# A mixture-of-experts block around attention: the first routing renumbered and regrouped, six weight splits moved into the expert loop

## Chip, cores and metric

The kernel runs on one core of a Trainium2 chip. The metric is device time in microseconds, the median of the runs; lower is better.

## What is computed

Two expert feed-forward layers, each added at half weight, stand around one attention layer. x is (8, 256, 256), 2048 tokens of width 256; there are 16 experts, 4 per token. Cut to what matters:

```
def ffn(x, ...):
    t = x * rsqrt(mean(x * x) + EPS) * norm_w
    logits = t @ gate_w.T + gate_b
    vals, idx = top_k(logits, 4)
    G[token, idx] = softmax(vals)
    h = einsum('mh,eoh->emo', t, w1) + b1
    a = minimum(h[..., ::2], 7); b = clip(h[..., 1::2], -7, 7)
    y = einsum('emi,edi->emd', a * sigmoid(1.702 * a) * (b + 1), w2) + b2
    return x + einsum('me,emd->md', G, y)
x = x + 0.5 * ffn(layernorm(x), ...)
x = x + attention(layernorm(x), ...)
x = x + 0.5 * ffn(layernorm(x), ...)
```

## The kernel before

The program is written out by hand for five engines, each with its own instructions in order and semaphores between them. It has these stages: the first routing (`route`), the first expert loop (`experts`), two batches of sums, attention with the second routing inside, the second expert loop, and the last sums (`combine`).

**Routing.** 2048 tokens are 16 tiles of 128, taken in 8 groups of 2. For each group ACT makes the normalised rows (`rows_made`, L628), PE turns them (L698), ACT copies them out (`turned`, L643), PE multiplies by the gate (L707), and DVE finds the four experts (`choice`, `orders`), waits for ACT's exponentials (L664) to make the gates (`weights`), and adds PE's ranks (L718, L720) to the count so far (`slots`, L549). POOL then sends every row of the tile four times by indirect DMA into the DRAM tensor `rows`, where each expert has a region of its own (`send`, L605): 64 sends. Beside that, the output bias is added to x for each group: PE turns the gates (L733), ACT copies them (`gates`, L649), PE multiplies by b2 and adds x (L738, L741), ACT copies the sum to x (`kept`, L655). At the end DVE makes a table of the 80 tiles of 128 rows over which the experts' regions are cut (`tile_columns`, `tile_lines`), SP and ACT write 16 pads (`pad_rows`, L331), and semaphore `s_tab` opens the loop.

**Splits.** PE's weights are used as a high and a low part. For experts 0 to 3 the raw weights are loaded right into the loop's rings; for 4 to 15 they go to one of three staging buffers (`load`, L373), ACT makes the high part (`high`, L384, three instructions), DVE the low part (`low`, L391, L393, three instructions), and the pair goes out to DRAM (`store`, L398), from where SP loads it in the loop. A load into a staging buffer waits until the store before it from this buffer has landed. 13 experts are split in the groups by `SHARE`, one behind them, 14 and 15 in the loop, at places that `HIGH_AT` and `LOW_AT` give.

**Expert loop.** 40 pairs of tiles. In step s the stages of different pairs lie side by side: PE turns the rows of pair s+1 (L914), ACT copies them (`th`, L1097), PE multiplies pair s by w1 (L947), DVE adds the bias (L1010), POOL clips (L1137), and so on up to `ys` (L1075), which POOL puts into `kbuf` by indirect DMA (L1129). ACT issues the fetches of the rows (`fetch`, L1064), four pairs ahead. In the first two pairs a fetch waits for the groups that its rows come from, from pair 2 on for all of them.

The order around the change is fixed by these hand-written sequences. In ACT's routing loop it is:

```
for g in range(NG):
    exponentials of g; stores and kept of g - 1; turned(g + 1)
    residual(g); gates(g); rows_made(g + 2); split.high of g + 1
```

The functions that the change touches:

## Time and profile before

| | |
|---|---|
| median of 3 runs | 855.37 us |
| the runs | 851.69, 855.37, 856.62 us |
| the profiled execution | 850.11 us |
| its span | 848.1 us |
| busy: PE, DVE, ACT, POOL | 86%, 69%, 51%, 47% of the span |
| longest share of the chain that ended last | PE 41% |

The page has a busy share for each engine, the span in 40 slices, the DMA queues (q1 is SP's, q10 ACT's, q0 POOL's), the chain of waits that ended last, and the costliest groups. The routing takes about the first 120 us of the span, the first loop the stretch to about 330 us.

### The profile page before, as it was taken

The numbers are of one execution on the slowest core, as the hardware profiler recorded it, in microseconds if no ns is written. First come the engines' busy times: TensorE is split into PE (matmuls) and PEld (weight loads), VectorE is DVE, ScalarE is ACT, GpSimd is POOL, SyncE is SP. The second block draws the span as 40 slices with busy tenths as digits, with TensorE's granted clock in tenths as the row PEclk, the third lists the DMA queues.
The fourth block names the chain that finished last, engine by engine and source line by source line (L and its number), as shares of the span: only waits on it lengthen the run. The fifth ranks groups of instructions, "written<-read, shape, count | busy, mean of one in ns | idle before, by whom it ended". The sixth has DMA issues, their size and how long they took to land.

```text
span 848.1 us, 17435 instructions
## 1 busy us (share of the span) xinstructions
PE 727.9 (86%) x4774; PEld 568.8 (67%) x4774; DVE 589.0 (69%) x1339; ACT 432.7 (51%) x922; POOL 399.5 (47%) x446
## 2 busy tenths in 40 slices
PE   2775559999999998789998889788489999999985
PEld 1443337888888887667776667556268888888872
DVE  5775638777777777477777577557587777777777
ACT  3664325555555555257655455453425555555551
POOL 6876722555454456333343441244614554455552
PEclk9999999999999999999997797789799999999998
DMA  7997978868887763544452223117555788787676
GB/s 303 364 387 290 353 240 332 305 217 261 271 293 259 247 215 119 197 151 158 146 194 107 106 107 114 43 56 252 192 182 194 262 270 270 249 255 245 214 259 230
DMA packets 87418, 188.86 MB, mean 223 GB/s; under 512 B 13072, under 2 KB 37920, under 8 KB 85792
## 3 DMA queue, kind: packets, MB, share of 16 engines
q1 hardware_dynamic: 46816, 105.55, 36.7%
q10 hardware_dynamic: 26736, 42.45, 15.1%
q0 software_dynamic: 13776, 39.75, 12.3%
q8 instruction: 46, 0.75, 0.4%
q14 instruction: 44, 0.36, 0.1%
HBM read 105.46 MB, written 65.45 MB: 202 GB/s over the span
## 4 chain that ended last, share of the span: by engine, by line
PE 41%; DVE 8%; issue 4%; another core or an unknown queue 3%; ACT 1%; DMA 1%; SPq 0%; POOL 0%; DVEq 0%; ACTq 0%
PE s_psT L947 13%; PE s_psG L971 6%; PE s_psO L1498 3%; PE s_psS L1463 3%; DVE s_a_nm L1731 3%; PE s_psS L914 2%; PE s_psG L1435 2%; PE s_psS L928 2%; PE s_psT L1479 2%; PE s_psT L1483 1%; PE s_psG L1545 1%; PE s_psG L1448 1%; PE s_psR L1570 1%; DVE all_x L2183 1%
## 5 line engine op out<-in xcount | busy, mean ns | idle before, releaser
L1129 POOL DMA_INDIRECT kbuf<-f_e_ys,f_e_place x79 | 79.7, 1009 | 91.3 <-ACT f_e_ys L1075 78.5
L1129 POOL DMA_INDIRECT kbuf<-s_e_own_ys,s_e_own_place x79 | 78.1, 989 | 92.9 <-ACT s_e_own_ys L1075 77.1
L1731 DVE TENSOR_REDUCE s_a_nm<-s_psS 128x4 f32<-128x1024 f32 x64 | 78.3, 1223 | 57.1 <-PE s_psS L1463 39.6
L947 PE MATMUL f_bank<-f_e_w,f_e_th 128*128 x316 | 113.7, 461 | 2.7 <-ACT f_e_th L1097 1.9
L947 PE MATMUL s_psT<-s_e_own_w,s_e_own_th 128*128 x316 | 112.6, 457 | 2.0 <-ACT s_e_own_th L1097 1.9
L1356 POOL DMA_INDIRECT rows<-s_a_row,s_a_slot_i x64 | 62.7, 980 | 105.5 <-DVE s_a_slot_i L1858 88.8
L1010 DVE TENSOR_TENSOR s_e_own_hb<-s_psT,s_e_own_bias 128x512 f32<-128x512 f32 x79 | 54.3, 688 | 45.0 <-PE s_psT L947 44.2
L1010 DVE TENSOR_TENSOR f_e_hb<-f_bank,f_e_bias 128x512 f32<-128x512 f32 x79 | 54.3, 687 | 44.9 <-PE f_bank L947 43.8
L1997 ACT ACTIVATE s_a_pT<-s_psT 128x1024 f32<-128x1024 f32 x62 | 63.3, 1022 | 43.2 <-PE s_psT L1483 34.2
L605 POOL DMA_INDIRECT rows<-f_r_row,f_r_slot_i x64 | 67.1, 1049 | 26.2 <-issue 18.5
L947 PEld LDWEIGHTS f_bank<-f_e_w,f_e_th 128*128 128x128 f32 x316 | 60.3, 191 | 23.5 <-issue 4.6
L947 PEld LDWEIGHTS s_psT<-s_e_own_w,s_e_own_th 128*128 128x128 f32 x316 | 59.5, 189 | 22.3 <-issue 3.4
L947 PE MATMUL s_psT<-s_e_own_w,s_e_own_tl 128*128 x158 | 55.5, 432 | 1.1 <-DVE s_e_own_tl L1024 1.1
L947 PE MATMUL f_bank<-f_e_w,f_e_tl 128*128 x158 | 55.9, 434 | 0.0
L1463 PE MATMUL s_psS<-s_a_ks,s_a_qs 64*128 64x256 f32 x256 | 34.7, 352 | 20.4 <-DVE s_a_nm L1731 19.9
L971 PE MATMUL f_bank<-f_e_w,f_e_ah 128*128 x316 | 50.9, 283 | 0.1
L971 PE MATMUL s_psG<-s_e_own_w,s_e_own_ah 128*128 x316 | 50.8, 283 | 0.1
L914 PE MATMUL f_bank<-all_ident,f_e_tb 128*128 128x128 f32 x160 | 43.0, 275 | 8.2 <-DMA f_e_tb<-rows 8.1
L1075 ACT ACTIVATE s_e_own_ys<-s_psG,s_e_tb 128x256 f32<-128x256 f32 x79 | 37.5, 474 | 21.1 <-PE s_psG L971 18.5
L971 PEld LDWEIGHTS f_bank<-f_e_w,f_e_ah 128*128 128x128 f32 x316 | 45.6, 188 | 3.5 <-issue 0.3
L971 PEld LDWEIGHTS s_psG<-s_e_own_w,s_e_own_ah 128*128 128x128 f32 x316 | 45.6, 188 | 3.3 <-issue 0.3
L1075 ACT ACTIVATE f_e_ys<-f_bank,f_e_tb 128x256 f32<-128x256 f32 x79 | 37.5, 474 | 19.5 <-PE f_bank L971 18.3
(379 smaller groups left out, 1849.6 us busy)
## 6 DMA issues: line engine op xcount, KB each, us to landing
w_split<-stage ACTq DMA_DIRECT2D x10, 1536.0 KB
f_e_w<-w_split SPq DMA_DIRECT2D x24, 512.0 KB
s_e_own_w<-w_split SPq DMA_DIRECT2D x24, 512.0 KB
f_e_tb<-rows ACTq DMA_DIRECT2D x80, 144.0 KB
s_e_tb<-rows ACTq DMA_DIRECT2D x80, 144.0 KB
stage<-w_raw SPq DMA_DIRECT2D x11, 768.0 KB
s_a_qs<-s_a_qk SPq DMA_DIRECT2D x32, 256.0 KB
s_a_ks<-s_a_qk SPq DMA_DIRECT2D x30, 256.0 KB
```

Of the source, the lines that this page charges most:

```text
L605: pool.indirect_dma_start(out=rows[:, :], out_offset=bass.IndirectOffsetOnAxis(ap=slot_i[i][:, t, k:k + 1], axis=0), in_=row[i][:, t, :], ...
L914: last = pe.transpose(psT[:, j, k * P:(k + 1) * P], tb[:, (2 * p + j) % (2 * RING), k * P:(k + 1) * P], c["ident"][:, :])
L947: last = pe.matmul(psH[j][:, :], left[:, p % 2, j, k * P:(k + 1) * P], w1[:, bass.ds(buf, 1), h, k * I2:(k + 1) * I2], start=n == 0, stop= ...
L971: last = pe.matmul(psY[j][:, 0:D], left[:, p % 2, j, k * P:(k + 1) * P], w2[:, bass.ds(buf, 1), h, o:o + D], start=n == 0, stop=n == len(p ...
L1010: dve.tensor_tensor(hb[:, p % 2, j, :], psH[j][:, :], bias[:, bass.ds(buf, 1), :].rearrange("p a n -> p (a n)"), ALU.add).then_inc(s_hb, 1)
L1075: act.activation(ys[:, n, :], psY[j][:, 0:D], ACT.Copy, scale=tb[:, slot, bass.ds(e + D, 1)]).then_inc(s_ys, 1)
L1129: pool.indirect_dma_start(out=kbuf[:, :], out_offset=bass.IndirectOffsetOnAxis(ap=place[:, n:n + 1], axis=0), in_=ys[:, n, :], in_offset=N ...
L1356: pool.indirect_dma_start(out=rows[:, :], out_offset=bass.IndirectOffsetOnAxis(ap=slot_i[i][:, t, k:k + 1], axis=0), in_=row[i][:, t, :], ...
L1463: last = pe.matmul(psS[:, (odd * QT + t) * S:(odd * QT + t + 1) * S], qs[i][rows, j, t * P:(t + 1) * P], ks[i][rows, j, :], start=True, st ...
L1498: last = pe.matmul(bank[h * VW:(h + 1) * VW, :], vz[:, b % 2, k, 4 * q + h, :], pT[:, (4 * n + h) % 8, k, :], start=k == 0, stop=k == QT - 1)
L1731: dve.tensor_reduce(nm[:, b % 2, :, :, j].rearrange("p t o -> p o t"), src, X_AXIS, ALU.max, negate=True).then_inc(s_mx, 1)
L1997: act.activation(to, score_bank(n)[:, :], ACT.Exp).then_inc(s_e, 1)
```

## The change

The four copies of a row are numbered by ascending expert instead of by size of the logit (`match_replace` and `max` on the slots take the place of `max_index` and one-hot products). POOL sends copies 0 and 1 of all tiles first, then all copies 2, then all copies 3: three stages. The first 7 pairs are fetched by SP (`early_fetch`), and each tile waits for the stage that its expert needs: expert 0 and 1 for the first, 2 for the second, all others for the third. Groups are 2, 4, 4, 4 and 2 tiles. Staging buffers are two instead of three; eight experts are split in the groups, 8 and 9 behind them, and 10 to 15 in loop steps 1 to 10. The clip of the first 14 pairs of the first loop moves from POOL to DVE. `gate` and `place` of a tile are copied out of the fetched rows as soon as they are there (`kept` in the loop, in both loops), so that the ring of fetched rows has 4 pairs instead of 8 and the fetch is 3 ahead; the rings of results have 16 places instead of 8. Rows of the whole routing stay in one buffer. The core of the diff:

```diff
-ROWS, ROWS1, RINGS = 3, 4, 8
+ROWS, RINGS = 3, 16
+GROUPS, X_PARTS = (2, 4, 4, 4, 2), (0, 2, 6)
 REAL = 3 * NT + 2 * NE
-NEED, EARLY = 3 * NT + 2 * NE + TOP * RINGS, 4
+NEED, EARLY = 3 * NT + 2 * NE + TOP * RINGS, 7
...
+class RoutedByRank:
+    def __init__(self, m):
+        self.s_scat, self.s_pad = [m.sem(f"scat{i}") for i in range(TOP - 1)], [m.sem(f"pad{i}") for i in range(2)]
+        self.s_tab, self.s_ends, self.s_real, self.s_landed = m.sem("tab"), m.sem("ends"), m.sem("real"), m.sem("landed")
+    def stage(self, k):
+        return max(0, k - 1)
+    def table(self, engine):
+        engine.wait_ge(self.s_tab, 1)
+    def landed(self, engine, stage):
+        engine.wait_ge(self.s_scat[stage], 16 * (2 * (T // P) + 1) if stage == 0 else 16 * (T // P))
+        if stage == 0:
+            engine.wait_ge(self.s_pad[0], 16 * FIRST)
+        engine.sem_inc(self.s_landed, 1)
+    def rows(self, engine):
+        engine.wait_ge(self.s_scat[0], 16 * (2 * (T // P) + 1))
+        engine.wait_ge(self.s_scat[1], 16 * (T // P))
+        engine.wait_ge(self.s_scat[2], 16 * (T // P))
...
+    if hist is None:
+        one.link(one.engine.tensor_scalar(tiles["need"][:, :], tiles["te"][:, :], 1.0, float(TOP - 1), ALU.max, ALU.min))
+        return
...
-    DIRECT, STAGED, PARTS = 4, 3, 3
-    FIRST = (4, 5, 0, 6, 1, 7, 2, 8, 9, 3, 10, 11, 12, 13, 14, 15)
+    DIRECT, STAGED, PARTS = 4, 2, 3
+    FIRST = (4, 5, 0, 1, 6, 2, 7, 3, 8, 9, 10, 11, 12, 13, 14, 15)
...
+    IN_CYCLE, AFTER = ((4,), (5, 0), (1, 6), (2, 7), (3,)), (8, 9)
...
-        for e in (4, 5, 0, 6, 1, 2, 3, 7, 8):
+        for e in (4, 5, 0, 1):
             split.load(sp, e)
         sp.wait_ge(s_bias, 16)
         first_biases(sp)
-        for e in (9, 10, 11, 12, 13):
+        for e in (2, 3, 6, 7):
             split.load(sp, e)
         sp.wait_ge(s_ends, 1)
         pad_rows(sp, m.phase, table, rows, c, s_pad, FIRST, some=range(NE - FIRST))
-        split.load(sp, 14)
+        for e in (8, 9):
+            split.load(sp, e)
...
+            for n in range(begin[g], begin[g] + GROUPS[g]):
+                for k in range(2):
+                    send(n, k)
+                if n in ROOTS_AFTER:
+                    inverse_roots(2 + ROOTS_AFTER.index(n))
+        for k in (2, 3):
+            for n in range(TT):
+                send(n, k)
+                if n == 3:
+                    routed.landed(pool, k - 2)
+        routed.landed(pool, 2)
...
+        rows_made(1)
+        for e in IN_CYCLE[0]:
+            split.high(act, e)
+        for g in range(LAST + 1):
             act.wait_ge(s_diff, g + 1)
+            act.activation(ex[:, 0:GROUPS[g], :], diff[:, 0:GROUPS[g], :], ACT.Exp).then_inc(s_ex, 1)
+            if g < LAST:
+                turned(g + 1)
             if g == 0:
                 act.wait_ge(s_one_more, 1)
                 act.dma_start(b_first, raw[:, :]).then_inc(s_bias, 16)
+            if g > 0:
+                stores(IN_CYCLE[g - 1])
+            if g < LAST:
+                for e in IN_CYCLE[g + 1]:
+                    split.high(act, e)
             residual(g)
+            if g + 2 <= LAST:
                 rows_made(g + 2)
+            if g > 0:
+                gates(g - 1)
+                kept(g - 1)
         act.wait_ge(s_ends, 1)
         pad_rows(act, m.phase, table, rows, c, s_pad, FIRST, some=range(NE - FIRST, NE))
+        split.high(act, AFTER[0])
+        gates(LAST)
+        kept(LAST)
+        stores(IN_CYCLE[LAST])
         act.activation(junk_s[:, :], c["zero"][:, 0:1], ACT.Sigmoid)
+        split.high(act, AFTER[1])
+        stores(AFTER[0:1])
...
+        def biases(g):
+            pe.wait_ge(s_gates, g + 1)
+            since(pe, s_gT, g)
+            for t in range(GROUPS[g]):
+                last = pe.transpose(psG[:, t * P:(t + 1) * P], row[:, begin[g] + t, D:D + NE], c["ident"][:, :])
+            last.then_inc(s_gp, 1)
+            pe.wait_ge(s_gT, g + 1)
+            pe.wait_ge(s_res, g + 1)
+            for h in halves(g):
+                since(pe, s_x, h)
+                for j in range(GPT):
+                    n = h * GPT + j
+                    t = n - begin[g]
+                    pe.matmul(psB[:, j * D:(j + 1) * D], gT[:, t * P:(t + 1) * P], c["b2"][:, :], start=True, stop=False)
+                    last = pe.matmul(psB[:, j * D:(j + 1) * D], c["ident"][:, :], x[:, n, :], start=False, stop=True)
+                last.then_inc(s_b, 1)
         all_there(pe)
         rows_turned(0)
         logits(0)
+        for g in range(LAST + 1):
+            ranks(g)
+            if g < LAST:
                 rows_turned(g + 1)
                 logits(g + 1)
+            if g > 0:
+                biases(g - 1)
+        pe.wait_ge(s_cols, 1)
+        tile_turns(pe, c, tiles, psN).then_inc(s_line, 1)
+        biases(LAST)
...
+    NBUF, NSEC, NY, RING, BANK, AHEADP, KEPT = 4, 5, RINGS, 4, 8, 3, 2 * RINGS
+    CLIP_FROM, BY_SP, BY_NEED = (14, EARLY, 0) if first_layer else (0, 0, 2)
...
+    HIGH_AT = {(1, 0): ((10, 0),), (1, 1): ((10, 1),), (2, 0): ((10, 2),), (3, 0): ((11, 0),), (3, 1): ((11, 1),), (4, 0): ((11, 2),),
+               (5, 0): ((12, 0), (12, 1)), (5, 1): ((12, 2),), (7, 0): ((13, 0), (13, 1)), (7, 1): ((13, 2),),
+               (8, 0): ((14, 0), (14, 1)), (8, 1): ((14, 2),), (10, 0): ((15, 0), (15, 1)), (10, 1): ((15, 2),)}
+    LOW_AT = {(1, 1): ((10, 0),), (2, 0): ((10, 1),), (2, 1): ((10, 2),), (3, 1): ((11, 0),), (4, 0): ((11, 1),), (4, 1): ((11, 2),),
+              (5, 0): ((12, 0),), (5, 1): ((12, 1), (12, 2)), (7, 0): ((13, 0),), (7, 1): ((13, 1), (13, 2)),
+              (8, 0): ((14, 0),), (8, 1): ((14, 1), (14, 2)), (10, 0): ((15, 0),), (10, 1): ((15, 1), (15, 2))}
+    STORE_AT, LOAD_AT, SECOND_LAG = {1: 9, 3: 10, 5: 11, 6: 12, 8: 13, 9: 14, 11: 15}, {0: 10, 2: 11, 4: 12, 6: 13, 7: 14, 9: 15}, 2
...
+        if p >= RING:
+            queue.wait_ge(s_tT, p - RING + 1)
+            queue.wait_ge(s_kept, p - RING + 1)
+        for j in range(2):
+            queue.wait_ge(routed.s_landed, need[j])
+            carry(queue, s_carry)
+        for j in range(2):
+            queue.dma_start(tb[:, (2 * p + j) % (2 * RING), :], rows[bass.ds(at(2 * p + j), P), :]).then_inc(s_tb[p % RING], 16)
...
+                dve.tensor_scalar(bc[:, b, :, :], hb[:, b, :, I1:I2], LIMIT + 1.0, 1.0 - LIMIT, ALU.min, ALU.max).then_inc(s_bc, 1)
```

Three places show how instructions move. The first is ACT in the routing: one cycle before (group 4, exponentials to exponentials; `f_r_gT` are the gates, `all_x<-f_bank` is `kept`).

```order
L664 ACTIVATE f_r_ex<-f_r_diff 128x32 [waits f1_r_diff]
L398 DMA w_split<-stage 128x3072 [waits f1_w_lo]
L655 ACTIVATE all_x<-f_bank 128x512 [waits f1_r_b]
L643 ACTIVATE f_r_tT<-f_bank 128x512 [waits f1_r_log,f1_r_tp]
L636 ACTIVATE all_x<-all_x,f_r_half,f_r_gain 128x256 [waits f1_r_row]
L636 ACTIVATE all_x<-all_x,f_r_half,f_r_gain 128x256
L649 ACTIVATE f_r_gT<-f_bank 16x256 [waits f1_r_b,f1_r_gp]
L628 ACTIVATE f_r_row<-all_x,f_r_shift,f_r_root 128x256 [waits f1_r_gp,f1_scat1,f1_r_norm]
L628 ACTIVATE f_r_row<-all_x,f_r_shift,f_r_root 128x256
L384 ACTIVATE stage<-stage,all_nw 128x512 [waits f1_w_in6]
L384 ACTIVATE stage<-stage,all_nw 128x512
L384 ACTIVATE stage<-stage 128x512
```

And one cycle of the changed kernel, group 3 of four tiles:

```order
L722 ACTIVATE f_r_ex<-f_r_diff 128x64 [waits f1_r_diff]
L690 ACTIVATE f_r_tT<-f_bank 128x512 [waits f1_r_log,f1_r_tp]
L437 DMA w_split<-stage 128x3072 [waits f1_w_lo]
L423 ACTIVATE f_e_w<-f_e_w,all_nw 128x512 [waits f1_w_in3]
L423 ACTIVATE f_e_w<-f_e_w,all_nw 128x512
L423 ACTIVATE f_e_w<-f_e_w 128x512
L682 ACTIVATE all_x<-all_x,f_r_half,f_r_gain 128x256 [waits f1_r_row]
L682 ACTIVATE all_x<-all_x,f_r_half,f_r_gain 128x256 x3
L698 ACTIVATE f_r_gT<-f_bank 16x512 [waits f1_r_b,f1_r_gp]
L705 ACTIVATE all_x<-f_bank 128x512 [waits f1_r_b] x2
L722 ACTIVATE f_r_ex<-f_r_diff 128x32 [waits f1_r_diff]
L437 DMA w_split<-stage 128x3072 [waits f1_w_lo]
```

The splits stood behind the copy of the gates and now stand ahead of it; the copy of the gates has only `kept`, which waits for PE's bias products, between it and the next exponentials.

The second place is PE at the end of the routing, from the end of the last ranks to the turning of the table's columns (`f_r_off` and those after it). Before:

```order
L718 MATMUL f_bank<-f_r_sent,all_before 128x16 [waits f1_r_slot,f1_r_sent]
L718 MATMUL f_bank<-f_r_sent,all_ones_b 128x16
L718 MATMUL f_bank<-f_r_sent,all_before 128x16
L720 MATMUL f_bank<-f_r_sent,all_ones_b 128x16 x2
L321 MATMUL f_bank<-all_ident,f_r_off 1x128 [waits f1_r_cols]
L321 MATMUL f_bank<-all_ident,f_r_te 1x128
L321 MATMUL f_bank<-all_ident,f_r_col 1x128
L321 MATMUL f_bank<-all_ident,f_r_need 1x128
L733 MATMUL f_bank<-all_ident,f_r_row 16x128 [waits f1_r_gT,f1_r_gates]
L733 MATMUL f_bank<-all_ident,f_r_row 16x128
L738 MATMUL f_bank<-all_b,f_r_gT 128x256 [waits f1_r_x,f1_r_gT]
```

Now:

```order
L778 MATMUL f_bank<-f_r_sent,all_ones_b 128x16 x2
L786 MATMUL f_bank<-all_ident,f_r_row 16x128 [waits f1_r_gT,f1_r_gates]
L786 MATMUL f_bank<-all_ident,f_r_row 16x128 x3
L795 MATMUL f_bank<-all_b,f_r_gT 128x256 [waits f1_r_x,f1_r_res,f1_r_gT]
L796 MATMUL f_bank<-all_x,all_ident 128x256
L795 MATMUL f_bank<-all_b,f_r_gT 128x256
L796 MATMUL f_bank<-all_x,all_ident 128x256
L795 MATMUL f_bank<-all_b,f_r_gT 128x256 [waits f1_r_x]
L796 MATMUL f_bank<-all_x,all_ident 128x256
L795 MATMUL f_bank<-all_b,f_r_gT 128x256
L796 MATMUL f_bank<-all_x,all_ident 128x256
L360 MATMUL f_bank<-all_ident,f_r_off 1x128 [waits f1_r_cols]
```

The bias products of the last group but one, for four tiles, stand between the last ranks and the table.

The third is SP's loads of raw weights in the routing. Before:

```order
L373 DMA stage<-w_raw 128x1536 [waits f1_w_out0]
L373 DMA stage<-w_raw 128x1536 [waits f1_w_out1]
L797 DMA f_e_bias<-b_first 128x512 [waits f1_r_bias]
L797 DMA f_e_bias<-b_first 128x512 x3
L373 DMA stage<-w_raw 128x1536 [waits f1_w_out2]
L373 DMA stage<-w_raw 128x1536 [waits f1_w_out0]
```

Now:

```order
L414 DMA f_e_w<-w_raw 128x1024
L415 DMA f_e_w<-w_raw 128x512
L414 DMA f_e_w<-w_raw 128x1024
L415 DMA f_e_w<-w_raw 128x512
L412 DMA stage<-w_raw 128x1536 [waits f1_w_out0]
L412 DMA stage<-w_raw 128x1536 [waits f1_w_out1]
```

The loads that wait for a store (`f1_w_out`) were five and had three buffers in turn; now there are two ahead of the pads, of experts 6 and 7, and each waits for the store of expert 4 or 5.

## Rows read from the trace of the kernel before

**Rows 1.** Timeline of DVE, loop: start us, us, instruction, count, [idle before <- releaser]

```profile
202.13 0.69 DVE L1010 TENSOR_TENSOR f_e_hb<-f_bank,f_e_bias 128x512 f32<-128x512 f32 x1 [1.27 <-PE f_bank L947]
...
207.23 0.69 DVE L1010 TENSOR_TENSOR f_e_hb<-f_bank,f_e_bias 128x512 f32<-128x512 f32 x1 [1.29 <-PE f_bank L947]
```

**Rows 2.** Timeline of ACT, from the routing into the loop

```profile
108.19 1.89 ACTq L331 DMA_DIRECT2D rows<-all_pad  x4
...
118.25 1.28 ACT L688 ACT_TABLE_LOAD   x1
...
121.86 0.60 ACT L1097 ACTIVATE f_e_th<-f_bank 128x512 fp32r<-128x512 f32 x1 [2.11 <-PE f_bank L914]
...
171.84 0.59 ACT L1097 ACTIVATE f_e_th<-f_bank 128x512 fp32r<-128x512 f32 x1
```

**Rows 3.** Timeline of POOL, routing

```profile
14.12 2.29 POOL L592 TENSOR_TENSOR f_r_root<-f_r_var,all_minus_half 128x12 f32<-128x12 f32 x1
...
19.06 1.06 POOL L605 DMA_INDIRECT rows<-f_r_row,f_r_slot_i  x1 [1.92 <-DVE f_r_slot_i L549]
20.43 0.96 POOL L605 DMA_INDIRECT rows<-f_r_row,f_r_slot_i  x1 [0.30 <-issue]
...
47.76 1.61 POOL L605 DMA_INDIRECT rows<-f_r_row,f_r_slot_i  x1 [0.30 <-issue]
...
112.48 0.97 POOL L605 DMA_INDIRECT rows<-f_r_row,f_r_slot_i  x1 [0.30 <-issue]
```

**Rows 4.** Timeline of DVE, routing and its end

```profile
18.90 0.28 DVE L566 TENSOR_SCALAR f_r_raw<-f_r_raw 16x256 f32<-16x256 f32 x1
...
47.84 0.68 DVE L393 TENSOR_TENSOR stage<-stage 128x512 fp32r<-128x512 f32 x1
...
98.55 0.29 DVE L549 TENSOR_REDUCE f_r_slot_i<-f_r_mix 128x8 int32<-128x128 f32 x1
...
115.12 0.15 DVE L579 COPY f_r_junk<-all_zero 128x1 f32<-128x1 f32 x1 [5.23 <-remote]
```

**Rows 5.** Timeline of PE, one group of two tiles

```profile
51.03 0.22 PE L718 MATMUL f_bank<-f_r_sent,all_before 128*128 128x16 bf16 x1
...
55.79 1.22 PE L738 MATMUL f_bank<-all_b,f_r_gT 16*128 16x256 f32 x2 [0.49 <-ACT f_r_gT L649]
...
60.25 0.22 PE L718 MATMUL f_bank<-f_r_sent,all_before 128*128 128x16 bf16 x1
...
60.43 1.09 PE L698 MATMUL f_bank<-all_ident,f_r_row 128*128 128x128 f32 x4
```

**Rows 6.** Timeline of ACT, routing

```profile
27.25 0.35 ACTq L398 DMA_DIRECT2D w_split<-stage  x1
...
40.80 0.72 ACT L384 ACTIVATE stage<-stage,all_nw 128x512 fp32r<-128x512 f32 x1 [4.18 <-DMA stage<-w_raw]
...
47.41 1.32 ACT L384 ACTIVATE f_e_w<-f_e_w,all_nw 128x512 fp32r<-128x512 f32 x2
...
52.84 1.08 ACT L636 ACTIVATE all_x<-all_x,f_r_half,f_r_gain 128x256 f32<-128x256 f32 x2
...
72.63 0.37 ACT L649 ACTIVATE f_r_gT<-f_bank 16x256 f32<-16x256 f32 x1 [7.83 <-remote]
```

**Rows 7.** Stretches: us, PE, PEld, DVE, ACT, POOL busy (x), PEclk, DMA, GB/s

```profile
17.00:94.00 77.00, 53.04 (x178) 31.90 (x178) 52.53 (x207) 44.80 (x90) 55.01 (x52) 1.00 0.92 353
...
132.00:147.00 15.00, 14.19 (x79) 10.76 (x78) 13.17 (x22) 6.42 (x14) 4.21 (x5) 1.00 1.00 376
```

**Rows 8.** Timeline of SP, routing

```profile
32.79 5.99 SPq L373 DMA_DIRECT2D stage<-w_raw  x2
...
101.11 17.63 SPq L331 DMA_DIRECT2D rows<-all_pad  x12
```

**Rows 9.** DMA issues: out<-in engine op count, KB, us to landing

```profile
all_x<-x_in SPq DMA_DIRECT2D x1, 256.0 KB, 3.3
```

**Rows 10.** Line 1064, durations ns min/median/max

```profile
L1064 ACTq MOVE f_e_tb<-rows x80: 29/35/38, 117.3 to 307.6; - x80
```

441 lines of the change are left out of this document (224 added, 217 removed).

## The prediction

> **What bounds the kernel now.** I read the stretches first, then the timelines of POOL, ACT, PE and DVE in the routing, then the steady loop. The first 120 us make no expert result; from then on PE is full. In the loop DVE waits for PE in every pair, and the pair repeats after 5.10 us (202.13 to 207.23) [rows 1]; what delays its start or one of its pairs moves the end by as much. ACT copies out the first rows (`th` of pair 0) at 121.86, and pair 10 at 171.84: 50.0 us for ten pairs, of which fewer than the last are full [rows 2].
>
> In the routing POOL's sends come 1.28 to 1.37 us apart when they need wait for nothing, and run from 19.06 to 113.4 [rows 3]; 64 of them are some 83 us, so copies sent in stages can save time only if the slots are there. The last slots are done at 98.55 + 0.29 = 98.8 [rows 4]. What makes the slots is a loop through PE and ACT: a group of two tiles repeats after 60.25 - 51.03 = 9.2 us, 4.5 of which (55.79 to 60.25) are the bias products [rows 5]. Eight groups at 9.2 from 15 on would end near 80; the rest are stalls: 4.2 us for a raw weight, 7.8 us in which ACT stood for nothing that the trace shows [rows 6], and others. DMA is at 0.92 there, 353 GB/s [rows 7]. So the questions are how long the new routing takes, and what the loop pays for the splits.
>
> **The new routing, step by step.** Durations: turning the rows 1.1 and bias products 4.5 for two tiles [rows 5]; ACT 0.54 for a tile of residual, as much for a tile of rows, 1.75 for a split's high part (two of three instructions are 1.32), 0.4 for the gates [rows 6], 0.6 for any copy of 128x512 [rows 2].
>
> *Start.* The shift of tiles 2 to 5 now stands ahead of the first choice, and needs POOL's root, which starts at 14.12 and took 2.29 for twelve values [rows 3]; eight give about 15.8. ACT then makes four rows (2.2) and a high part (1.75) before the first exponentials at 20.2, so the first slots come at 22 (now 18.8). Through the roots of the next part, behind four sends, the copies for group 2 end at 35.
>
> *The cycle.* For four tiles ACT now does, in order: high parts (1.75 or 3.5), residual 2.2, rows 2.2, gates 0.4, and waits for PE's bias products with a copy between the halves (4.5 + 0.6 + 4.5 = 9.6), then 0.6; only then come the next exponentials, ranks and turned rows (0.6 + 2.2 + 1.2). With 3.5 that is 22.5 us where two groups now take 18.4. The splits used to lie under the bias products; now nothing does.
>
> *The two staging buffers.* ACT issues the store of expert 4 at 35, and its next high part but one, of expert 6, needs a load that waits for this store. The store issued at 27.25 let SP go on at 32.79: 5.5 us [rows 6, 8]. The load then took until 40.80, 8.0 us, beside a second one; I take 6.0, between 3.3 (what 256 KB of x took [rows 9]) and 8.0. By the Trainium skill, DMA: Bandwidth & Descriptors, Anatomy of one DMA, a transfer costs about 2 us and its bytes at 436 GB/s; for 1.57 and 0.79 MB that gives an estimate of 5.6 and 3.8 us, and the sum would be 2.2 us less at each place. No row shows such a load alone.
> So expert 6 starts at 46.7; +1.75 +2.2 +2.2 +0.4 = 53.3; the first bias products (two tiles) and the copy 58.4; ranks, rows and copies 61.8. The store of expert 5 goes there: +5.5 +6.0 = 73.3 for expert 7; +1.75 +2.2 +1.1 +0.4 = 78.8; +9.6 = 88.4; group 4's rows 90.7; +1.75 +2.2 +0.4 = 95.1; +9.6 +0.6 = 105.3; exponentials, gates and slots 2.7: **last slots at 108**, 9 us later than now.
>
> *To the loop.* Then ACT has residual and gates (1.5), waits for the biases of group 3 (9.6 +0.6 = 117.2), loads registers and issues four pads (2.6; 1.89 is the row [rows 2]), high part of 8 (1.75), gates 0.4, products 4.5, copy 0.6, the table load and its dummy 1.5, high part of 9 (1.75): `th` of pair 0 at **131**, now 121.86: **+9**. The first stage has landed long before (last slots +4 sends +4 more, 119), and the table is there at 119, so the earlier fetch by SP buys nothing. I count no unexplained stall, though there were 7.8 and 5.2 us [rows 4, 6]; under less DMA they may be gone, or come again (0 to 12 more). SP's pads took 17.6 us [rows 8], up to 12 of it waiting; here they have till 120.
>
> **The loop.** DVE's free time in a pair is 1.27 us [rows 1]. The clip of the first 14 pairs costs it between 0.28 (its scalar operation on 256 columns [rows 4]) and 0.69 (two-input operations of this width [rows 1]); I take 0.6. What is left, 0.67, holds one low part (0.64 apart). Steps 2 and 4 have two, 5, 7, 8 and 10 have three: 2 x 0.6 + 4 x 1.25, less 1.3 that steps 6 and 9 give back: **+5**. ACT has as many parts and is less full. The extra copies of `kept` are two short ones a pair on an engine that is busy 51%: nothing, and nothing in the second loop.
> DMA: from 108 to `th` of pair 10 must move, by the shapes: 36 sends and 16 pads of 0.147 MB, raw weights 8 to 15 (6.3), stores 7 to 14 (12.6), 13 pairs of rows (3.8), results (1.8), weights of experts 4 to 6 (4.5): 36.7 MB, of which 6.6 (the last store, weights fetched early) need not be in time. At 376 GB/s, a full stretch of the loop [rows 7], 30.1 MB are 80 us and 36.7 are 98; the time there is 131 + 50 + 5 - 108 = 78. So 2 to 20 more; and each raw weight has one step from its load to its high part, behind a 1.57 MB store on the same queue. I take 4: loop **+9**, between 5 and 25.
> Sixteen rings instead of eight add eight waits with a count behind each of two last planes; 16 instructions at 0.035 [rows 10] are 0.56, twice: **+1**.
>
> **Sum.** 9 + 9 + 1 = +19 on the profiled execution's own 850.1: 869. The median shown is 855.4, 5.3 above that execution; on its scale **874 us**. A difference of 0.5% (4.3 us) is about what a measurement can tell from no change.
>
> **Rivals.**
> *The loads are in time, no difference* (0.15). If experts 6 and 7 are there when ACT comes (38.7, 63.6), the waits of 5.8 and 9.7 us go, `th` is at 115.5, and the loop pays its 5: -6.4 +5 +1, 855. For it: DMA carries half the load up to there. Against: two buffers, and rows of 5.5 and 8.0.
> *Faster* (0.22): the loads are in time, and the biases don't hold the next group, since ACT and PE were held by DMA stalls and not by each other; each of the two full cycles gives back 4.1. -6.4 -8.2 +1, and the loop takes 0 to 5: 842 to 847 on the median's scale. It decides at last slots before 88. The 7.8 us at ACT speak for it, the 9.2 us cycles, which show PE and ACT in turn, against.
> *DMA decides* (0.10): all 36.7 MB must pass; loop +25, 890.
> *Sends held up by DVE* (0.05). The send at 47.76 took 1.61 us instead of 0.97, beside DVE's low part at 47.84 with two inputs [rows 3, 4]. If each of 32 sends in the loop pays 0.64, copies 3 land at 108 + 5 + 41 + 20 = 174, and pair 7, for which ACT waits in step 5, has its rows near 178 instead of 166: +10, 884. This is the lock of the Trainium skill, SBUF — State Buffer, Who interferes with whom: a VectorE instruction with two SBUF inputs, or in a two-port mode, and a GpSimd one that reads SBUF shut each other out; the moved clip is a candidate for such a mode. The trace agrees, with 0.64 us for one send.
> *It doesn't do what it says*: ACT's fetch of pair 7 waits for all copies, so only seven pairs gain from the stages; that is in the sum.
>
> **Chances.** The forecast holds 0.48 (862 to 886). Faster by over 0.5%: the 0.22 and 0.02 of the case in which the loads are in time; within: the other 0.13 of that case; slower: 0.48 + 0.10 + 0.05 = 0.63. The range goes down to 843, which leaves out about half of the faster case (0.11), and up to 892, past which lies the upper half of the DMA case and a little of the forecast (0.08).
>
> **What would show it.** Right: the last slots after 100; ACT waiting for w_raw in groups 1 and 2; ACT idle 9 us before each `kept` of four tiles; `th` of pair 0 after 125; more than 55 us for ten pairs, with DVE or DMA near full. Wrong: slots before 90, no wait of ACT for raw weights, or ten pairs in 50 us; then the time is under 855.

## Result and profile after

The changed kernel takes **935.5 us** (median of 4 runs, 930.0 to 937.8), the kernel before beside it 854.8: a ratio of **1.096** (95% interval 1.089 to 1.103). The record has a fifth run, 943.2 us, that is not in the median. The profiled execution spans 928.1 us, that of before 848.1.

The kernel before itself took about 855 us beside some of the experiments and about 805 us beside others; I call these the 855 level and the 805 level, and this result is of the first.

Where the 80.0 us are, read at `th` (ACT's first copy of a pair's rows) in both traces. The column on the right is from later profiles of the same two kernels at the 805 level (experiments 9 and 10):

| part | before | after | difference | 805 level |
|---|---|---|---|---|
| last slots | 98.8 | 102.3 | +3.5 | 91.9 to 102.2, +10.3 |
| `th` of pair 0 | 121.9 | 136.1 | +14.2 | 114.2 to 130.1, +15.9 |
| pairs 0 to 10 | 50.0 | 92.6 | +42.7 | 51.8 to 77.8, +26.0 |
| pairs 10 to 20 | 50.6 | 58.0 | +7.4 | +10.9 |
| pairs 20 to 39 | 96.4 | 104.2 | +7.8 | +2.5 |
| between the loops | 301.0 | 303.7 | +2.7 | -0.8 |
| second loop, pairs 0 to 39 | 195.3 | 201.4 | +6.0 | +7.0 |
| behind it | 32.9 | 32.0 | -0.9 | -0.7 |

First ACT's `th` in the changed kernel's timeline, the rows that answer to [rows 2]: pairs 0, 1, 2, 7 and 10.

```profile
136.10 0.60 ACT L1224 ACTIVATE f_e_th<-f_bank 128x512 fp32r<-128x512 f32 x1 [6.20 <-issue]
...
153.34 0.60 ACT L1224 ACTIVATE f_e_th<-f_bank 128x512 fp32r<-128x512 f32 x1 [15.79 <-remote]
...
162.64 0.60 ACT L1224 ACTIVATE f_e_th<-f_bank 128x512 fp32r<-128x512 f32 x1 [6.72 <-PE f_bank L1011]
...
198.68 0.60 ACT L1224 ACTIVATE f_e_th<-f_bank 128x512 fp32r<-128x512 f32 x1 [3.30 <-PE f_bank L1011]
...
228.74 0.59 ACT L1224 ACTIVATE f_e_th<-f_bank 128x512 fp32r<-128x512 f32 x1
```

The loop starts badly (17.2 us between pairs 0 and 1, after an idle time that the trace can put down to no engine) and then runs at 5 to 12 us a pair (5.0 a pair before). Two engines say what stood around the start: SP, which now fetches the first rows, and POOL with its late sends.

SP's timeline:

```profile
112.45 1.20 SPq L412 DMA_DIRECT2D stage<-w_raw  x2
129.40 14.70 SPq L940 DMA_DIRECT2D f_e_tb<-rows  x4
147.60 1.41 SPq L877 DMA_DIRECT2D f_e_w<-w_split  x2
153.23 11.52 SPq L940 DMA_DIRECT2D f_e_tb<-rows  x10
```

SP's register instructions in front of a fetch, in the stretch from 102 to 152 (durations in ns, min/median/max):

```profile
L911 SPq FUSED_REGOPS  x4: 16/693/698, 127.3 to 140.6; - x4
```

POOL's first send of the last group and the last send of all:

```profile
102.58 1.11 POOL L646 DMA_INDIRECT rows<-f_r_row,f_r_slot_i  x1 [5.09 <-DVE f_r_slot_i L592]
...
149.02 0.97 POOL L646 DMA_INDIRECT rows<-f_r_row,f_r_slot_i  x1 [0.30 <-issue]
```

POOL sends for 47 us without a pause (0.3 us between two sends, once 1.3). In that time SP needs 0.69 us for a register instruction that takes 0.04 from 153.2 on, so that four fetches take 14.7 us. PE turned the rows of pair 1 at 143.1 to 143.7; ACT's copy of them starts at 153.34, 3.3 us behind the last send. PE's timeline:

```profile
143.08 0.66 PE L1011 MATMUL f_bank<-all_ident,f_e_tb 128*128 128x128 f32 x4 [1.32 <-DMA f_e_tb<-rows]
```

The kernel before has the same thing in small: its pads on SP took 17.6 us, and the sends beside them ended at 113.5 [rows 3, 8], and its 7.8 and 5.2 us of "remote" idle lie beside sends [rows 4, 6].

The stretch that answers to the loop's first part, PE busy 53.9 of 80 us at a granted clock of 0.78 (before, from 120 to 200: 75.9 at 1.00), with DMA at 0.72, and one part of it:

```profile
150.00:230.00 80.00, 53.92 (x250) 41.42 (x251) 46.14 (x76) 33.17 (x94) 11.73 (x12) 0.78 0.72 264
...
190.00:200.00 10.00, 3.75 (x12) 2.81 (x13) 4.24 (x8) 2.59 (x8) 1.95 (x2) 0.60 0.95 391
```

No compute engine is full there. The 16 DMA engines are not full on average, but they are in parts: 0.93 from 170 to 180 and 0.95 from 190 to 200. At the 805 level, where the late sends lie beside a loop that already runs, they are full for the loop's first 30 us, with PE busy 23.2 of them:

```profile
130.00:160.00 30.00, 23.18 (x97) 16.48 (x98) 19.56 (x32) 12.22 (x40) 16.09 (x17) 0.94 0.99 368
```

ACT's timeline over one step of it shows the pattern of pairs 6 to 10:

```profile
193.94 0.34 ACTq L437 DMA_DIRECT2D w_split<-stage  x1
194.38 0.47 ACT L1199 ACTIVATE f_e_ys<-f_bank,f_e_gate 128x256 f32<-128x256 f32 x1 [1.20 <-DVE stage L432]
...
202.10 0.34 ACTq L412 DMA_DIRECT2D stage<-w_raw  x1
...
204.23 1.97 ACTq L1169 DMA_DIRECT2D f_e_tb<-rows  x4
```

The load of a raw weight (202.10) waits for the store before it (193.94) to land, and the fetch of pairs 8 and 9 (204.23) stands behind that load on ACT. The code issues it late, too: pair 7 is fetched in step 5 and pair 8 in step 6, one step before PE turns them, and the later pairs two steps before. PE's timeline has the other end, rows of pairs 7 and 8 that come late:

```profile
196.25 0.47 PE L1011 MATMUL f_bank<-all_ident,f_e_tb 128*128 128x128 f32 x1 [6.49 <-DMA f_e_tb<-rows]
...
208.04 0.33 PE L1011 MATMUL f_bank<-all_ident,f_e_tb 128*128 128x128 f32 x1 [3.76 <-DMA f_e_tb<-rows]
```

The second loop has waits of its own (the waits from 600 to 900 us; before, 0.3 us in all):

```profile
PEld s_psS L1011 <- DMA s_e_tb<-rows: 8.2, 9, 2.4
...
PE s_psS L1011 <- DMA s_e_tb<-rows: 5.3, 6, 2.1
```

### The profile page after: what moved, and what is told of

It reads as the page before. It is cut to its first block, busy times and chain, and to the rows that moved or that the text cites. A ratio compares the mean times of both kernels' runs of the same rounds, so it can differ in the third digit from the quotient of the medians.

```text
span 928.1 us, 17820 instructions
## 1 busy us (share of the span) xinstructions
PE 748.2 (81%) x4786; PEld 580.1 (63%) x4786; DVE 583.8 (63%) x1324; ACT 446.8 (48%) x1074; POOL 390.9 (42%) x433
## 4 chain that ended last, share of the span: by engine, by line
PE 33%; DVE 7%; another core or an unknown queue 4%; DMA 4%; issue 3%; ACT 3%; ACTq 1%; DVEq 0%; POOL 0%
PE s_psT L1044 9%; PE s_psG L1068 4%; DMA s_e_tb<-rows 4%; PE s_psO L1622 3%; PE s_psS L1587 2%; DVE s_a_nm L1855 2%; PE s_psG L1559 2%; PE s_psS L1011 2%; PE s_psS L1025 2%; PE s_psT L1603 1%; PE s_psT L1607 1%; PE s_psG L1572 1%; PE s_psG L1669 1%; PE s_psR L1694 1%
## 5 line engine op out<-in xcount | busy, mean ns | idle before, releaser
L1044 PE MATMUL f_bank<-f_e_w,f_e_th 128*128 x316 | 123.9, 489 | 12.8 <-ACT f_e_th L1224 11.5
L1480 POOL DMA_INDIRECT rows<-s_a_row,s_a_slot_i x64 | 62.9, 983 | 102.9 <-DVE s_a_slot_i L1982 84.3
L1044 PEld LDWEIGHTS f_bank<-f_e_w,f_e_th 128*128 128x128 f32 x316 | 65.0, 206 | 35.6 <-issue 18.5
L1011 PE MATMUL f_bank<-all_ident,f_e_tb 128*128 128x128 f32 x160 | 46.0, 294 | 36.0 <-DMA f_e_tb<-rows 27.1
L1199 ACT ACTIVATE f_e_ys<-f_bank,f_e_gate 128x256 f32<-128x256 f32 x79 | 37.5, 475 | 65.9 <-PE f_bank L1068 38.8
L1199 ACT ACTIVATE s_e_own_ys<-s_psG,s_e_own_gate 128x256 f32<-128x256 f32 x79 | 37.6, 475 | 59.3 <-PE s_psG L1068 45.3
L1044 PE MATMUL f_bank<-f_e_w,f_e_tl 128*128 x158 | 59.5, 459 | 0.0
L1068 PE MATMUL f_bank<-f_e_w,f_e_ah 128*128 x316 | 51.8, 287 | 0.3 <-issue 0.3
L1025 PE MATMUL f_bank<-all_ident,f_e_ac 128*128 128x128 f32 x160 | 44.1, 285 | 7.0 <-DVE f_e_al L1115 7.0
```

What stands on the lines that cost most here:

```text
L1011: last = pe.transpose(psT[:, j, k * P:(k + 1) * P], tb[:, (2 * p + j) % (2 * RING), k * P:(k + 1) * P], c["ident"][:, :])
L1025: last = pe.transpose(psA[:, j, k * P:(k + 1) * P], ac[:, p % 2, j, k * P:(k + 1) * P], c["ident"][:, :])
L1044: last = pe.matmul(psH[j][:, :], left[:, p % 2, j, k * P:(k + 1) * P], w1[:, bass.ds(buf, 1), h, k * I2:(k + 1) * I2], start=n == 0, stop= ...
L1068: last = pe.matmul(psY[j][:, 0:D], left[:, p % 2, j, k * P:(k + 1) * P], w2[:, bass.ds(buf, 1), h, o:o + D], start=n == 0, stop=n == len(p ...
L1199: act.activation(ys[:, n, :], psY[j][:, 0:D], ACT.Copy, scale=gate[:, i % KEPT:i % KEPT + 1]).then_inc(s_ys, 1)
L1480: pool.indirect_dma_start(out=rows[:, :], out_offset=bass.IndirectOffsetOnAxis(ap=slot_i[i][:, t, k:k + 1], axis=0), in_=row[i][:, t, :], ...
```

## Experiments

All ratios are to the kernel before beside the same run. It took 855.9 us beside experiments 1 to 4, 805.6 beside 5 to 8, 805.8 beside 9 to 12, 804.4 beside 13 to 16 and 854.6 beside 17 and 18. Times of a part are from one profiled execution of each kernel. "Pairs a to b" is the time between their `th`.

### The start: 1 to 4, 8 to 10

**1. All copies sent at once.**
```diff
-                for k in range(2):
+                for k in range(TOP):
                     send(n, k)
...
-        for k in (2, 3):
-            for n in range(TT):
-                send(n, k)
...
```
POOL's roots also move, to behind tiles 0 and 2 instead of 1 and 3.

> The changed kernel, but POOL sends all four copies of a tile as soon as its slots are there, and the stages are told of only after the last. Theory A (what stands between 114 and 153 us is caused by POOL's unbroken row of 36 late sends: SP takes 0.70 us for each instruction, and PE's signals reach ACT and DVE late): the last send ends near 114, SP's first instructions take 0.05 us again, `th` of pair 0 starts at 124 to 130 and that of pair 1 within 7 us of it (136.1 and 153.3 in the changed kernel): 20 to 28 us less, 908 to 916. Theory B (the loop pays for its splits and its ring anyway, whatever the start): pair 1 comes early as well, but pair 10 stays near 225: under 8 us less.

Ratio 1.077 (1.070 to 1.084), 921.4 us: neither theory's number (908 to 916, or under 8 us less). The last send ends at 120.6, but pair 0 comes at 142.7, later than 136.1. ACT's timeline and POOL's last send show why:

```profile
109.95 0.60 ACT L701 ACTIVATE all_x<-f_bank 128x512 f32<-128x512 f32 x1 [5.93 <-issue]
123.38 0.60 ACT L701 ACTIVATE all_x<-f_bank 128x512 f32<-128x512 f32 x1 [12.83 <-remote]
```
```profile
119.60 0.97 POOL L646 DMA_INDIRECT rows<-f_r_row,f_r_slot_i  x1 [0.30 <-issue]
```

The unbroken row of sends now lies over the end of the routing, and ACT's copy behind PE and SP's pads are held up there; ACT's 12.8 us end 2.8 us behind the last send. Once it is over, pair 1 follows after 5.9 us. So the slowness goes with the sends again, and moving them does not remove it.

**2. ACT fetches the first rows, as before the change.**
```diff
-    CLIP_FROM, BY_SP, BY_NEED = (14, EARLY, 0) if first_layer else (0, 0, 2)
+    CLIP_FROM, BY_SP, BY_NEED = (14, 0, EARLY) if first_layer else (0, 0, 2)
```


> The changed kernel, but the rows of pairs 0 to 6 are fetched by ACT, with the same waits for their stages, instead of SP; the order of the sends is kept. If only SP is slowed by the sends: `th` of pair 0 at 132 to 134 and of pair 1 at 138 to 141, 10 to 14 us less in all. If PE's signals are late too (theory A in full): pair 1 or 2 still starts only after POOL's last send, near 150, and the gain is under 5 us. If the tiles really wait for late stages: `th` of pair 1 stays at 153 and there is no gain.

Ratio 1.076 (1.069 to 1.083). ACT's timeline:

```profile
143.69 10.22 ACTq L940 DMA_DIRECT2D f_e_tb<-rows  x4
153.96 0.60 ACT L1224 ACTIVATE f_e_th<-f_bank 128x512 fp32r<-128x512 f32 x1 [13.32 <-remote]
```

Pair 1 still starts at 154, whoever fetches: it is not SP alone. ACT's own instructions are now the slow ones, 0.70 us each from 140.9 to 153.5, and 0.05 before and behind:

```profile
L911 ACTq FUSED_REGOPS  x3: 697/699/704, 140.9 to 152.1; - x3
```

The gain by the medians (16 us) comes behind it, pairs 1 to 10 in 60.7 us instead of 75.4, and is larger than expected. Of these 14.7 us, 8.4 lie between pairs 6 and 8, whose rows ACT here fetches one step earlier than in the changed kernel, and 5.1 at pair 2, whose rows no longer stand behind the weights of expert 4 in SP's queue (see 15).

**3. A pause behind each late send.**
```diff
                 send(n, k)
+                pool.tensor_scalar(rest[:, :], row[:, n, 0:256], LIMIT + 1.0, 1.0 - LIMIT, ALU.min, ALU.max).then_inc(s_paused, 1)
+                pool.wait_ge(s_paused, (k - 2) * TT + n + 1)
```


> The changed kernel, but behind each of the 32 late sends POOL does one short operation on a scratch tile and waits for it, so that the sends come about 1.8 to 2.2 us apart instead of 1.28. Theory A with the sends' closeness as the cause: SP's instructions between 114 and 150 take 0.05 us, `th` of pair 0 at 126 to 131 and of pair 1 at 132 to 138, though the sends end near 175; pairs from 7 on wait for the last stage then: total between 15 less and 5 more. If the stages are what the pairs wait for: pair 1 starts at 170 or later and the kernel is 15 to 25 us slower.

Ratio 1.074 (1.064 to 1.084), against 1.096, although the sends come 1.74 us apart and end at 165.6 instead of 150.0. SP's and ACT's timelines:

```profile
118.29 2.08 SPq L943 DMA_DIRECT2D f_e_tb<-rows  x4
...
128.33 17.82 SPq L943 DMA_DIRECT2D f_e_tb<-rows  x10
```
```profile
128.55 0.57 ACT L1227 ACTIVATE f_e_th<-f_bank 128x512 fp32r<-128x512 f32 x1
134.71 0.60 ACT L1227 ACTIVATE f_e_th<-f_bank 128x512 fp32r<-128x512 f32 x1 [5.21 <-issue]
```

Four fetches take 2.1 us instead of 14.7, pair 1 starts 18.6 us earlier. Sends that are further apart and end later make an earlier start: theory A, as expected. The time between the loops is 302.2 us here, so it is the pause and not the 805 level that made SP fast.

**4. A ring of 7 pairs in the second loop.**
```diff
-RING, ..., AHEADP = 4, ..., 3
+RING, ..., AHEADP = 4 if first_layer else 7, ..., 3 if first_layer else 4
```

> The changed kernel, but in the second loop alone the ring of fetched rows holds 7 pairs instead of 4 and ACT fetches 4 pairs ahead instead of 3. Theory: the second loop is 6.1 us longer than before because rows come late: it loses PE's waits for rows (s_e_tb), 201.4 back to 195 to 197, 4 to 6 us less in all. Rival (the two short copies a pair on ACT, or the scratch ring of results, cost it): no change.

Ratio 1.092 (1.086 to 1.098). The second loop takes 194.5 us instead of 201.4, and PE's waits for rows are gone (waits from 700 to 900 us):

```profile
PEld s_psS L1011 <- DMA s_e_tb<-rows: 0.7, 1, 0.7
...
PE s_psS L1011 <- DMA s_e_tb<-rows: 0.3, 1, 0.3
```

The ring is the cause, and 201.4 is the shortest of its kind: the second loop takes 201.4 to 214.6 us in the ten changed kernels with a ring of 4, 194.4 to 200.2 in the six with a ring of 7, and 193.6 to 198.7 in the four traces of the kernel before and its variants. By the medians only 2 to 3 us are gained: in the profiled execution pair 0 came at 150.5, with SP slow again, 14 us later than in the changed kernel's own; the start varies that much at this level.

**8. The pause in the kernel before**, behind the sends of its last three groups.
```diff
+                    if g >= 5:
+                        pool.tensor_scalar(rest[:, :], row[i][:, t, 0:256], LIMIT + 1.0, 1.0 - LIMIT, ALU.min, ALU.max).then_inc(s_paused, 1)
+                        pool.wait_ge(s_paused, ((g - 5) * GPT + t) * TOP + k + 1)
```

> The kernel before, with a short operation of POOL and a wait for it behind each send of the last three groups (24 sends). Theory A (sends without a gap slow SP and delay PE's signals to ACT and DVE): SP's pads, 17.6 us before, take 7 or less, ACT's last copies come at 112 to 113 instead of 115.9, `th` of pair 0 at 115 to 120 instead of 121.9: 846 to 853. Rival (in the kernel before, the sends themselves set the start): the last send comes some 10 us later, near 123, and the kernel is 2 to 8 us slower.

Ratio 1.009 (1.006 to 1.012): the rival. It ran at the 805 level, where SP is not slowed at all, so the pause could only cost: the last send ends at 122.0 (108.2 without), and pair 1 waits for it (127.1, pair 0 111.1). Whether it helps at the 855 level was not tried.

**9 and 10. Both kernels as they are**, at the 805 level.

> The changed kernel as it is, once more: the kernel before took 855.9 us beside the first four experiments and 805.6 beside the next four, and SP showed 0.70 us for each instruction during POOL's sends only beside the first. Theory C (that slowness belongs to the chip or its state and adds to what the change costs): where the kernel before takes some 805 us, the changed one has `th` of pairs 0 and 1 at 129 and 135, without the 17 us between them, and is at 1.065 to 1.075 of the kernel before. Rival (the gap between pairs 0 and 1 is the change's own, through SP's fetch): 153 for pair 1 again, and 1.09 or more.

> The kernel before as it is, for its profile beside the same chip. If the slowness belongs to the chip: SP's pads take 6 to 8 us instead of 17.6, `th` of pair 0 at 110 to 118; the first ten pairs 50 us as before; what shrinks most is the attention between the loops (301 us from the first loop's last pair to the second's first, to near 260).

Ratio of the changed kernel 1.084 (1.079 to 1.088). Its SP (register instructions, then timeline) and its ACT:

```profile
L911 SPq FUSED_REGOPS  x14: 44/44/51, 117.4 to 140.8; - x14
```
```profile
117.56 2.54 SPq L940 DMA_DIRECT2D f_e_tb<-rows  x4
```
```profile
130.15 0.57 ACT L1224 ACTIVATE f_e_th<-f_bank 128x512 fp32r<-128x512 f32 x1
136.22 0.60 ACT L1224 ACTIVATE f_e_th<-f_bank 128x512 fp32r<-128x512 f32 x1 [5.13 <-PE f_bank L1011]
...
207.98 0.59 ACT L1224 ACTIVATE f_e_th<-f_bank 128x512 fp32r<-128x512 f32 x1
```

The same sends, 1.28 us apart until 149.3, and no slow SP, no late signal; in the kernel before the time between the loops is 259.3 us instead of 301.0, and DVE's 16.6 us of "remote" idle at the softmax are 0. Theory C holds: the slowness belongs to the state of the device, and not to the change. The change has more sends at the wrong place and so pays more for it there, 1.096 against 1.084 (above the 1.065 to 1.075 expected). The larger part of the loss is at both levels.

### The routing: 6

**6. Three staging buffers** instead of two, with eight rings of results for the room.
```diff
-    DIRECT, STAGED, PARTS = 4, 2, 3
+    DIRECT, STAGED, PARTS = 4, 3, 3
...
-        for e in (4, 5, 0, 1):
+        for e in (4, 5, 6, 0, 1):
...
-LOAD_AT ... {0: 10, 2: 11, 4: 12, 6: 13, 7: 14, 9: 15}
+LOAD_AT ... {-1: 10, 0: 11, 2: 12, 4: 13, 6: 14, 7: 15}
```


> The changed kernel with three staging buffers instead of two (room from eight rings of results instead of sixteen, and small tiles that share memory), raw weights 6 and 8 loaded one buffer earlier and those of 10 to 15 one or two steps earlier in the loop. Theory (two buffers hold ACT up in the routing, 7.7 and 7.1 us, and in the loop): last slots near 92 instead of 102.3, pairs 2 to 10 in 54 to 60 us: 12 to 20 less. Rival (the bias products of four tiles hold ACT and PE just as long when the raw weight is there): last slots at 98 or later and under 6 less.

Ratio 1.072 (1.066 to 1.078), 805 level. The high part of expert 7, in the changed kernel and here:

```profile
68.09 1.33 ACT L423 ACTIVATE stage<-stage,all_nw 128x512 fp32r<-128x512 f32 x2 [7.08 <-DMA stage<-w_raw]
```
```profile
56.63 1.32 ACT L423 ACTIVATE stage<-stage,all_nw 128x512 fp32r<-128x512 f32 x2
```

Last slots at 90.8 and pair 0 at 114.9, against 91.9 and 114.2 in the kernel before at this level: two buffers are nearly the whole of the later start. But the loop takes half of it back: pairs 0 to 10 in 86.0 us instead of 77.8. Pair 2 waits 13.9 us behind pair 1, since SP waits for the weights of expert 4 to land before it fetches it; pairs 2 to 10 take 66.0 us (68.8 with two buffers, 54 to 60 expected). So a third buffer is worth 15 us in the routing and 3 in the loop.

### The loop: 5, 7, 11 to 18

**5, 13, 14. Parts of the splits left out.** In 5 and 13 experts 10 to 15 use the split weights of 4 to 9; in 14 raw weights are stored.
```diff
+    def have(e):
+        return e - 6 if e > 9 else e
...
-w_split[e, :, part, 0:HID]
+w_split[have(e), :, part, 0:HID]
...
```
5: `HIGH_AT`, `LOW_AT` and `LOAD_AT` empty, one store left. 13: high and low parts kept, `LOAD_AT` empty, one store. 14: loads and stores kept, each store waiting for its load; `HIGH_AT` and `LOW_AT` empty.

> The changed kernel without the splits of experts 10 to 15: no load, high part, low part or store in the loop but the store of expert 9; experts 10 to 15 use the split weights of 4 to 9 in both loops. It bounds what the six splits cost in the loop. Theory (the loop of the changed kernel is long because ACT stands behind stores and loads and DVE's low parts): pairs 2 to 10 take 42 to 48 us instead of 66, 18 to 24 us less in all. Rival (rows that come late and a lower granted clock after the slow start make the pairs long, splits or not): 56 us or more, under 10 less.

> The changed kernel with the 18 high and 18 low parts of experts 10 to 15 in the loop as they are, on what lies in the staging buffers, but without their loads and stores (both loops use the weights of experts 4 to 9 for 10 to 15). It parts the cost of the splits in the loop: with all of it pair 0 to pair 10 is 77.9 us, with none 58.1. If DVE's and ACT's own time and the lockstep of PE, DVE and ACT decide: 68 to 76. If the transfers (raw weight behind the store behind the split, on ACT's queue) decide: 58 to 64.

> The other half: the changed kernel with the loads and stores of experts 10 to 15 in the loop, each store waiting for its load, and without their high and low parts (raw weights are stored). Pair 0 to pair 10: if the transfers decide, 70 to 78 us; if ACT's and DVE's work does, 58 to 66. If each alone gives 65 or less, it is their chain (load, high, low, store, load) and no single part.

| kernel (805 level) | pairs 0 to 10 | pair 10 at | ratio |
|---|---|---|---|
| before | 51.8 | 166.0 | 1 |
| changed, no split in the loop (5) | 58.1 | 189.8 | 1.056 (1.052 to 1.060) |
| high and low parts only (13) | 68.1 | 198.3 | 1.065 (1.060 to 1.070) |
| loads and stores only (14) | 72.6 | 202.7 | 1.084 (1.075 to 1.093) |
| changed | 77.8 | 208.0 | 1.084 (1.079 to 1.088) |

The splits cost 19.7 us in the first ten pairs. The work of ACT and DVE alone costs 10.0, the transfers alone 14.5; they overlap in part. The first is at the edge of what was expected if the work decides, the second within what was expected if the transfers do; neither half is the cause by itself, and 65 or less for each, which would have spoken for their chain alone, did not come. DMA is full over the first 30 us of the loop in 9 and in 14 (0.99 in both). In 5 it is full over the first 20 (1.00), and pair 4 comes 17.3 us behind pair 0 (19.0 in the kernel before), so a full DMA alone does not make the pairs long. In 14 the time as a whole is no shorter, although pair 10 is 5.3 us earlier and the profiled span 1.5 less; its interval is wide. Without any split 6.3 us of the 26.0 remain, and pairs 7 and 8 still come 9 us apart, with PE waiting 3.2 and 2.9 us for their rows. All copies have landed long before: ACT's timeline of 5 has the fetch of pair 7 at

```profile
163.49 0.88 ACTq L1166 DMA_DIRECT2D f_e_tb<-rows  x2
```

and the last send ended at 149.9. What makes these rows late is the step in which the code fetches them, not the stage that they wait for.

**7. The ring of 7 pairs, 4 fetched ahead, in both loops**, with eight rings of results.
```diff
-ROWS, RINGS = 3, 16
+ROWS, RINGS = 3, 8
...
-RING, ..., AHEADP = 4, ..., 3
+RING, ..., AHEADP = 7, ..., 4
```

> The changed kernel with 7 pairs of rows in the ring instead of 4 and 4 fetched ahead instead of 3, in both loops, and with eight rings of results instead of sixteen. Theory: the steady parts lose their waits for rows: pairs 10 to 30 of the first loop take 103 to 108 us instead of 116.6, the second loop 195 to 197 instead of 201 to 210: 10 to 18 less. Rival (the first loop's steady part is long for another reason): only the second loop is shorter, 5 to 8 less.

Ratio 1.058 (1.053 to 1.063), 0.026 under the changed kernel. Pairs 10 to 30 take 108.3 us instead of 115.1 (102.9 before), pairs 20 to 39 97.0 instead of 99.4 (96.9 before), the second loop 200.2 instead of 203.8 (196.8 before). Pairs 0 to 10 take 79.3: nothing gained there. The profiled span is 12.6 us shorter, and these stretches (pairs 10 to 39 and the second loop) are 11.3 of it. The rings of results changed with it; 4, which leaves them, shows the same in the second loop.

**11. The store behind `ah`**, not at the start of ACT's step.
```diff
-            if first_layer and s in STORE_AT:
-                split.store(act, STORE_AT[s])
             if pair(s - 4):
                 scaled(s - 4, 1)
...
             high_parts(s, 0)
+            if first_layer and s in STORE_AT:
+                split.store(act, STORE_AT[s])
```

> The changed kernel, but in each step of the loop that stores a split expert ACT issues the store behind `ah` and the high part, not at the step's start. Theory D (ACT at the start of a step waits for DVE's low parts, which stand at the end of DVE's step behind PE, so that PE, DVE and ACT run in lockstep): the waits of ACT for DVE's low part, 9.5 us, go, pairs 3 to 10 take 50 to 57 us instead of 61: 5 to 12 us less than the changed kernel beside it. Rival (the raw weight's load behind the store behind the split sets the step, wherever ACT stands): under 3 less, or longer, since the store and so the next load go out later.

Ratio 1.093 (1.088 to 1.098) against 1.084 (1.079 to 1.088), pairs 3 to 10 in 67.3 us instead of 61.4. The rival is right: with two buffers the next load waits for this store, and a later store makes the loop slower.

**12. Ring of 7, late store, pair 2 fetched by SP and pairs 7 to 10 by ACT earlier.** The edits of 7 and 11, and:
```diff
-            for p in range(2):
+            for p in range(3):
                 early_fetch(sp, at, p, landed[2 * p:2 * p + 2], s_carrys)
...
-{BY_SP - 2: (BY_SP,), BY_SP - 1: (BY_SP + 1, BY_SP + 2)}
+{BY_SP - 3: (BY_SP, BY_SP + 1), BY_SP - 2: (BY_SP + 2,), BY_SP - 1: (BY_SP + 3,)}
```

> All that helped or should: the ring of 7 pairs fetched 4 ahead and eight rings of results (the kernel a_ring7), the store behind `ah`, the rows of pair 2 fetched by SP ahead of the weights of expert 4, and the rows of pairs 7 to 10 fetched one to two steps earlier by ACT. If the losses are separate: 1.035 to 1.045 of the kernel before. If one bound (splits on two buffers) holds the first ten pairs: as a_ring7, 1.055 to 1.06. It does not come under 1.02 if the late stages and the splits are the change's own price.

Ratio 1.057 (1.054 to 1.060), as 7. Pair 7 now follows pair 6 after 6.1 us instead of 12.6, so the earlier fetch removes the loss there. But pair 10 is at 204.1 instead of 208.3, and pair 20 at 265.6 (264.6 in 7). What is gained at one pair is lost again behind it; that it is the splits which take it back was expected, but is not shown.

**15, 16. Three buffers, the ring of 7 in the second loop, earlier fetches; and that with the late store.** The edits of 6 and 4, SP's `range(3)` of 12, in 16 also that of 11, and:
```diff
-                return {BY_SP - 2: (BY_SP,), BY_SP - 1: (BY_SP + 1, BY_SP + 2)}.get(s, ())
+                return (s + AHEADP,) if s + AHEADP >= BY_SP else ()
```

> The kernel a_three_staged (three staging buffers, eight rings of results; last slots at 90.8, th of pair 0 at 114.9) and, on top, the ring of 7 pairs in the second loop, SP's fetch of pair 2 ahead of the weights of expert 4, and ACT's fetches of pairs 7 and 8 one step earlier. Theory: the 13.9 us between pairs 1 and 2 become 4, the 12.3 between pairs 6 and 7 become 9 or less, the second loop 196 to 200: 1.072 becomes 1.04 to 1.05. Rival (the late sends, whose last lands near 142, set pair 7, and the rest waits less elsewhere): over 1.055.

> The kernel a_three_fetch with the stores behind ah and the high part of their step. With two buffers the late store cost 8 us, since the next load waits for it. With three the load has a step more: if the lockstep at the step's start is the loss, pairs 3 to 10 take 8 to 12 us less than in a_three_fetch; if the late store only moves the wait, the same within 3 us.

Ratios 1.045 (1.040 to 1.049) and 1.045 (1.039 to 1.052): the best of this family, and the late store changes nothing once there are three buffers. Pair 2 follows pair 1 after 2.9 us, and the same loss appears at pair 3. SP's and PE's timelines of 15:

```profile
114.49 1.66 SPq L876 DMA_DIRECT2D f_e_w<-w_split  x2
126.58 7.43 SPq L939 DMA_DIRECT2D f_e_tb<-rows  x8
```
```profile
133.89 0.48 PE L1010 MATMUL f_bank<-all_ident,f_e_tb 128*128 128x128 f32 x1 [7.21 <-DMA f_e_tb<-rows]
```

SP stands 10.4 us behind the weights of expert 4, and the rows of pair 3 behind SP. DMA is full there too (1.02 from 120 to 130).

**17. The clip of 14 pairs on DVE, in the kernel before.**
```diff
+            if first_layer and pair(s) and s < 14:
+                ...
+                dve.tensor_scalar(bc[:, b, :, :], hb[:, b, :, I1:I2], LIMIT + 1.0, 1.0 - LIMIT, ALU.min, ALU.max).then_inc(s_bc, 1)
             low_parts(s, 1)
...
-            if pair(s - 1):
+            if pair(s - 1) and not (first_layer and s - 1 < 14):
```

> The kernel before with the clip of the first 14 pairs on DVE instead of POOL, nothing else. The prediction had 0.6 us a pair where a low part stands beside it and nothing elsewhere: pair 0 to pair 14 within 2 us of the kernel before, 0 to 2 us slower in all. Rival (DVE's clip waits behind hb and delays the next hidden rows of each pair): 0.5 us a pair or more, 7 us slower.

Ratio 1.001 (0.997 to 1.005): the clip costs nothing that can be measured in this loop; pairs 0 to 10 take 51.4 us (50.0 before). Its cost beside the low parts of six experts was not tried by itself.

**18. As 15, pair 3 fetched ahead of the weights too.**
```diff
-            for p in range(3):
+            for p in range(4):
```

> The kernel a_three_fetch, but SP fetches the rows of pair 3 too ahead of the weights of expert 4, whose landing it waits for (12 us). If that wait is a loss of its own: th of pair 3 at 129 to 131 instead of 136.3, pair 10 at 180 to 184 instead of 187.5, the kernel at 1.037 to 1.042 instead of 1.0445. Rival (the splits on the path of pairs 4 to 10 take the time up again): pair 10 at 186 or later, and the same time.

It ran at the 855 level: 1.056 (1.050 to 1.062), so it does not compare with 1.045. There SP was slow from about 95 to 141 and pair 1 came 18.3 us behind pair 0. Pair 3 came 4.8 us behind pair 2, and pair 4 then 13.4 us behind pair 3, as PE's timeline shows:

```profile
160.86 0.48 PE L1010 MATMUL f_bank<-all_ident,f_e_tb 128*128 128x128 f32 x1 [8.94 <-DMA f_e_tb<-rows]
```

The wait has moved to the first pair behind the weights once more. What the time would be at the 805 level is open.

## Why the prediction was wrong

It said 874 us, 843 to 892, slower with 0.63; 935.5 was measured. The direction was right and the routing nearly so; the loop was not.

- **The routing: right in its mechanism.** First slots at 22.2 (said 22), copies for group 2 at 35.8 (35), waits for the raw weights of experts 6 and 7 of 7.7 and 7.1 us (5.8 and 9.7), bias products standing open behind them, last slots at 102.3 (108). From a store's issue to the next load's took 6.3 and 5.1 us (said 5.5), from there to the weight 4.2 and 4.8, where 6.0 was taken. The estimate by the Trainium skill, DMA: Bandwidth & Descriptors, Anatomy of one DMA, was 5.6 and 3.8: for the load it was the nearer. That section of the Trainium skill is about transfers issued by GpSimd; ACT issued these stores and SP these loads. Experiment 6 shows the two buffers as the cause. One slip in the working: its times for expert 6, ready at 46.7 and wanted at 38.7, are 8.0 apart and not 5.8; the forecast does not use the difference, and the measured 7.7 fits the 8.0.
- **`th` of pair 0 at 131: met at the 805 level (130.1), 5 us short at the 855 level (136.1).** The hit has luck in it. The slots came 6 us earlier than said, and ACT then waited once more for a raw weight, that of expert 8, which the prediction had nowhere (7.1 us at the 805 level, 6.6 here, in ACT's timeline):

```profile
119.18 1.33 ACT L423 ACTIVATE stage<-stage,all_nw 128x512 fp32r<-128x512 f32 x2 [6.63 <-DMA stage<-w_raw]
```

  "The earlier fetch by SP buys nothing" held at the 805 level, where the rows are there before ACT is. At the 855 level it cost, because SP crawls beside the sends. The rows that warned were on the table: SP's pads at 17.6 us and 7.8 and 5.2 us of unexplained idle [rows 4, 6, 8]. The prediction set them at nothing, "0 to 12 more", and did not ask what they had in common, though it knew that 36 sends would now stand behind the last slots.
- **The loop, +9: the step that failed.** Pairs 0 to 39 cost 57.9 us more at the 855 level, 39.4 at the 805 level. The term of the sum that was mis-sized is the price of the splits in the loop: DVE's time (+5) and DMA's bytes (+4) were added as two small loads. In the first ten pairs the six splits cost 19.7 us (5), the work of ACT and DVE alone 10.0 (13) and the transfers alone 14.5 (14). Two things stand there together. DMA is full for the loop's first 30 us at the 805 level (0.99, against 0.82 in 5), so the prediction's own bound of 25 (all 36.7 MB must pass), near the 26.0 measured for ten pairs, cannot be called right or wrong in its reason. And the work hangs in a chain: a raw weight's load waits for the store of two experts earlier, the store for DVE's low part, that for ACT's high part, that for its load, and all of ACT's part lies in its queue in front of `ys`, `sg`, `th` and the fetches. One sentence of the prediction named it ("each raw weight has one step from its load to its high part"), but the sum gave it no price. The late store (11) shows that the chain counts; a third buffer gave only 3 us in the loop (6). How the 19.7 us divide between the full DMA and the chain no run here shows. The clip was priced in the +5 and costs nothing in the kernel before (17).
- **The first pairs at the 855 level: a term put at nothing.** Pair 1 came 17.2 us behind pair 0 (6.1 at the 805 level). The pause (3) takes the gap away.
- **Fetches of pairs 7 and 8: not in the sum.** They are issued one step later than the others; with the earlier fetch the time from pair 6 to pair 8 falls from 23.0 to 14.6 us (2) and from 22.9 to 14.7 (12).
- **"Nothing in the second loop": wrong.** The diff cuts the ring of fetched rows from 8 pairs to 4 and the distance from 4 to 3, and the prediction looked only at the two short copies that make this possible. It is worth 6.8 us in the second loop at the 855 level (4), and 7 us of pairs 10 to 30 at the 805 level (7).
- **Only seven pairs gain from the stages: the reason was wrong.** Fetches from pair 7 on do wait for all copies, and these land about 150; but the fetch of pair 7 is issued at 191.6, at 170.3 in 9 and at 163.5 in 5, long after that. Its rows come late by its place in ACT's order.
- **Sixteen rings, +1:** the time between the loops is 2.7 us longer at one level and 0.8 shorter at the other. Not resolved.
- **The rivals.** *Loads in time* and *faster* fell with the slots at 102. *DMA decides* is not excluded for the first ten pairs: DMA is full there for 30 us, and the transfers alone cost 14.5 (14). Its 890 us left out the rest of the loss. *Sends held up by DVE*: one send, at 120.76 beside DVE's low part of expert 8, took 1.43 us instead of 0.97, as [rows 3] had it; but the late sends end at 149.3 at the 805 level, beside a loop that already runs, and at 150.0 at the 855 level, where DVE stood idle. It decides nothing.

The mean granted clock of the first ten pairs, 0.78 against 1.00, is part of the loss and not a cause of its own: it was 1.00 until PE fell idle at 143.7, and 0.50, the lower of TensorE's two levels (1.2 and 2.4 GHz), from 146 on, while PE did next to nothing until 160. How much of the loss is clock was not separated.

## What to carry to other kernels

When work moves into a loop that has room on every engine, draw the chain that it makes (load, split, store, next load) with its number of buffers, and set its length against the loop's period; sums of busy time did not show it here. Read DMA's share in stretches as short as the waits: a mean of 0.84 hid 30 us at 0.99. Here a wait on ACT's or SP's queue held up everything behind it, so look at what stands behind each store, load or fetch that moves to another engine, and in which step the last ones are issued. A smaller ring or a shorter distance of fetching ahead is a part of a change like any other, and is priced in every loop that uses it.

## What was not expected of the hardware

At the 855 level a row of indirect sends by POOL, 1.28 us apart without a gap, went with SP at 0.69 us an instruction instead of 0.04 (the kernel before: up to 0.71), and a copy of ACT came up to 10 us behind the work of PE that it waited for; both ended 2 to 4 us behind the last send. Where ACT had fetches to issue beside the sends (2), ACT's instructions took 0.70 us as well; the few that it had in the changed kernel, at 137, took 0.05. Whether PE's signals are late or ACT is slow to act on them, no run separates. A pause of 0.4 us in each 1.74 us removed it (3). At the 805 level the same sends did nothing of the kind (9). What lies behind it no run here shows, nor that it belongs to one chip: the record numbers the chips 3, 14, 10, 2 and 2 for experiments 1 to 4, 5 to 8, 9 to 12, 13 to 16 and 17 and 18, so number 2 stands at both levels. The two levels of the kernel before, 855 and 805 us, differ by 42 us in the attention between the loops, where the 855 level shows the same unexplained idle.
